# Three PSUM banks for the attention maxima, one shared bank for the transposes, and a new order of ticks, in a fused perceiver layer on one Trainium2 core

## The reference, cut to what matters

```python
Q = (q @ Wq + bq);  K = k @ Wk + bk;  V = v @ Wv + bv        # K, V: [2048, 32], shared by the heads
attn = softmax(Q K^T * scale);  out = (attn V) @ Wo + bo
```

## Time and profile before

| | us |
|---|---|
| median of 3 runs | 2032.25 |
| lowest, highest | 2029.79, 2034.01 |
| the profiled execution's own time | 2033.48 |
| its span | 2031.7 |
| PE, DVE, ACT, POOL busy | 1985.8, 1253.5, 1123.3, 1599.4 |

### The profile page before, as it was taken

One profiled execution on the slowest core, in us unless ns is written; L12 is line 12 of the kernel. 1 busy time (PEld: TensorE's weight loads), 2 busy tenths in 40 slices (PEclk: granted clock), 3 DMA queues, 4 the chain that ended last, 5 costly groups with the idle time before them and its releaser, 6 DMA issues. The chain is left out here.

```text
span 2031.7 us, 34305 instructions
## 1 busy us (share of the span) xinstructions
PE 1985.8 (98%) x12396; PEld 1310.8 (65%) x12396; DVE 1253.5 (62%) x2218; ACT 1123.3 (55%) x2093; POOL 1599.4 (79%) x1387
## 2 busy tenths in 40 slices
PE   7899999999999999999999999999999899999998
PEld 4436565656565555656565656556556899999998
DVE  5666777767777777777777777776753333333333
ACT  3656666666666666656666666666553233333333
POOL 0798999999898989899998989898995155555555
PEclk7789999999999999999999999999999899999999
DMA  6524131312213131312122121301200399999994
GB/s 227 187 104 147 44 107 38 89 49 77 79 63 89 37 89 37 108 37 88 37 87 69 55 82 58 88 32 41 78 6 17 139 366 358 355 356 354 354 363 168
DMA packets 105129, 262.23 MB, mean 129 GB/s; under 512 B 8576, under 2 KB 33920, under 8 KB 96256
## 3 DMA queue, kind: packets, MB, share of 16 engines
q1 hardware_dynamic: 96624, 236.04, 33.9%
q10 hardware_dynamic: 4752, 13.50, 1.8%
q0 software_dynamic: 3584, 10.49, 1.3%
HBM read 223.67 MB, written 25.72 MB: 123 GB/s over the span
## 5 line engine op out<-in xcount | busy, mean ns | idle before, releaser
L854 DVE TENSOR_REDUCE mpart<-bank 128x1 f32<-128x512 f32 x1024 | 670.5, 684 | 241.0 <-PE bank L434 236.6
L679 ACT ACTIVATE weights<-bank 128x512 f32<-128x512 f32 x1024 | 585.0, 597 | 238.5 <-PE bank L447 228.2
L1061 POOL TENSOR_TENSOR psum<-psum,weights 128x512 f32<-128x512 f32 x384 | 490.8, 1278 | 3.8 <-ACT weights L679 2.4
L1061 POOL TENSOR_TENSOR podd<-podd,weights 128x512 f32<-128x512 f32 x384 | 491.1, 1279 | 3.3 <-ACT weights L679 3.3
L447 PE MATMUL bank<-qT,kT 97*128 97x512 f32 x1024 | 481.9, 480 | 4.4 <-ACT weights L679 3.8
L434 PE MATMUL bank<-kT,qT 96*128 96x512 f32 x1024 | 447.0, 455 | 5.7 <-DVE mpart L854 4.1
L434 PEld LDWEIGHTS bank<-kT,qT 96*128 96x128 f32 x1024 | 198.4, 194 | 152.3 <-DVE mpart L854 99.2
L447 PEld LDWEIGHTS bank<-qT,kT 97*128 97x128 f32 x1024 | 194.3, 192 | 117.4 <-ACT weights L679 59.8
L459 PE MATMUL bank<-weights,v 128*32 128x512 f32 x2048 | 264.4, 612 | 0.0
L1317 POOL TENSOR_TENSOR w2l<-w,w2h 128x1024 fp32r<-128x1024 f32 x64 | 202.9, 3171 | 75.9 <-PE ebank L1230 54.5
L1260 ACT ACTIVATE hh<-ebank 128x512 fp32r<-128x512 f32 x64 | 38.2, 597 | 223.4 <-PE ebank L1214 223.4
(11 more groups left out here) (172 smaller groups left out, 3000.9 us busy)
## 6 DMA issues: line engine op xcount, KB each, us to landing
w<-in_w SPq DMA_DIRECT2D x48, 2048.0 KB, 20.1
w_first<-in_ctx SPq DMA_DIRECT2D x64, 1024.0 KB, 5.1
w_first<-in_w SPq DMA_DIRECT2D x16, 2048.0 KB, 11.6
dispatched<-route ACTq DMA_DIRECT2D x17, 513.0 KB, 4.2
dis<-dispatched SPq DMA_DIRECT2D x16, 513.0 KB, 3.5
qT<-qh SPq DMA_DIRECT2D x124, 64.0 KB, 4.5
xin<-in_x SPq DMA_DIRECT2D x16, 256.0 KB, 2.9
qT<-qs SPq DMA_DIRECT2D x64, 64.0 KB, 2.1
```

The source lines that it names most:

```text
L679: e.activation(p[n % NP], B_BANK[u % 2][:], ACT.Exp).then_inc(p_act.sem, 1)
L854: e.tensor_reduce(mpart[g % 2][:, 4 * (n % 4) + n // 4:4 * (n % 4) + n // 4 + 1], max_bank(b, g, n)[:], AX.X, ALU.max).then_inc(max_dve.se ...
L1061: e.tensor_tensor(acc[:], first, p[(UNITS * b + u) % NP], ALU.add).then_inc(psum_pool.sem, 1)
```

## The change

The bank of transposes is gone. Its bank (5) becomes a third bank of maxima, and the transposes of x and values take their turn in `KV_BANK`, in the same chain as keys, queries and sums. The quads of a group, before at ticks 20, 20, 33 and 37 from the group's start, are now at 21, 21, 33 and 33. All tables of ticks are new. No arithmetic, no instruction and no transfer is added or dropped; instructions change their bank, their place and their waits.

```diff
-STEADY = Prep(norm=-54, norm_pool=-47, xn=-29, xnt=-7, xnt_act=11, qproj=[28, 29, 31, 40], q_dve=38, q_act=42,
-              q_pool=43, qsend=52, kv=[21, 44, 57, 74], kvlow=[21, 45, 57, 79], kvs=[19, 44, 60, 78], kh=[23, 50,
-              65, 80], kl=[22, 52, 72, 81], vt=[59, 94], vt_act=[86, 96])
+STEADY = Prep(norm=-59, norm_pool=-40, xn=-11, xnt=8, xnt_act=13, qproj=[37, 41, 42, 48], q_dve=51, q_act=52,
+              q_pool=67, qsend=58, kv=[22, 53, 76, 86], kvlow=[23, 51, 76, 86], kvs=[26, 58, 83, 96], kh=[31, 64,
+              82, 97], kl=[32, 66, 87, 99], vt=[72, 106], vt_act=[74, 123])
+FIRST = Prep(norm=4, norm_pool=4, xn=5, xnt=6, xnt_act=7, qproj=[13, 14, 15, 16], q_dve=15, q_act=16, q_pool=18,
+             qsend=19, kv=[7, 8, 16, 40], kvlow=[8, 10, 16, 71], kvs=[8, 11, 17, 19], kh=[9, 12, 64, 80], kl=[10,
+             12, 65, 80], vt=[61, 126], vt_act=[66, 117])
-PE_AT = dict(sums=11, x1=[22, 24, 25, 27], xn2T=34, V=[38, 39, 40, 41], rkT=44, I=49, X1=52, Vn=100, oT2=103,
-             x2=[107, 109, 110, 112], xn3T=123, lg=126, loc=134, Y=[56, 62, 69, 78, 89, 96], Z=[57, 65, 73, 83, 92,
-             97], XT=[59, 68, 74, 84, 94])
+PE_AT = dict(sums=17, x1=[22, 23, 26, 30], xn2T=39, V=[43, 45, 46, 47], rkT=49, I=52, X1=53, Vn=113, oT2=116,
+             x2=[119, 120, 121, 122], xn3T=132, lg=135, loc=141, Y=[57, 70, 81, 87, 97, 106], Z=[61, 75, 84, 90,
+             100, 109], XT=[67, 76, 85, 95, 105])
+DVE_AT = dict(recip=[12, 13, 14, 15], att=17, x1=30, XT1=52, MT=53, IT=53, x2=124, lg=134, oh=135, row=139, Y=[58,
+              68, 81, 88, 96, 104], Z=[64, 69, 84, 92, 98, 104])
+POOL_AT = dict(xb=4, norm2=27, x12=30, rn=33, MT0=42, XT1=46, norm3=122, row=178)
-MAX_AT = [-37, -35, -34, -33, -32, -30, -28, -27, -24, -23, -19, -18, -14, -14, -11, -9]
-MAX_DVE = [-39, -37, -37, -36, -36, -30, -29, -28, -24, -23, -21, -21, -16, -14, -12, -12]
-MAX_TURN, MAX_ROW, PV_AT = -6, -7, [20, 20, 33, 37]
+MAX_AT = [-39, -39, -36, -35, -33, -30, -28, -27, -26, -25, -22, -19, -17, -14, -13, -12]
+MAX_DVE = [-38, -37, -35, -34, -32, -31, -30, -28, -27, -25, -21, -21, -20, -12, -12, -9]
+MAX_TURN, MAX_ROW, PV_AT = -8, -9, [21, 21, 33, 33]
...
-        A_BANK, B_BANK, PV_BANK, T_BANK, KV_BANK, P_BANK = bank[0:2], bank[2:4], bank[4], bank[5], bank[6], bank[7]
+        A_BANK, B_BANK, PV_BANK, KV_BANK, P_BANK = [bank[0], bank[1], bank[5]], bank[2:4], bank[4], bank[6], bank[7]
...
             + [(TICKS * (b - 1) + prep(b).qproj[0], b, ("q", 0)) for b in range(B)]
+            + [(TICKS * (b - 1) + prep(b).xnt, b, ("x", 0)) for b in range(B)]
+            + [(TICKS * (b - 1) + t, b, ("v", m)) for b in range(B) for m, t in enumerate(prep(b).vt)]
             + [(TICKS * (b + 1) + PE_AT["sums"], b, ("s", 0)) for b in range(B)])]
...
-            return [*A_BANK, P_BANK][n % 3] if b == g == 0 else A_BANK[(17 * g + n) % 2]
+            return A_BANK[(17 * (HG * b + g) + n) % 3]
...
+                if max_read(b, g, n) is not None:
+                    e.wait_ge(*max_read(b, g, n))
...
-                    transposes(T_BANK, lambda j: xin[:, j * P:(j + 1) * P]).then_inc(xnT_pe.sem, 1)
+                    transposes(KV_BANK, lambda j: xin[:, j * P:(j + 1) * P]).then_inc(xnT_pe.sem, 1)
...
-                    if b:
+                    if b or c == 0:
                         e.wait_ge(*kv_read(b, ("k", c)))
```

More of the change, by code:

```diff
@@ new lines @@
+LOAD_AFTER, W1_AT, ZERO_AT, ZERO_STEP = 4, 80, 34, 12
+PE_AT = dict(sums=17, x1=[22, 23, 26, 30], xn2T=39, V=[43, 45, 46, 47], rkT=49, I=52, X1=53, Vn=113, oT2=116,
+             x2=[119, 120, 121, 122], xn3T=132, lg=135, loc=141, Y=[57, 70, 81, 87, 97, 106], Z=[61, 75, 84, 90,
+             100, 109], XT=[67, 76, 85, 95, 105])
+ACT_AT = dict(xn2=36, ss=38, rk=45, xn2T=38, V=47, rkT=49, X1=52, Vn=112, oT2=113, xn3=129, xn3T=132, eg=134, X=[67,
+              77, 84, 94, 102])
+DVE_AT = dict(recip=[12, 13, 14, 15], att=17, x1=30, XT1=52, MT=53, IT=53, x2=124, lg=134, oh=135, row=139, Y=[58,
+              68, 81, 88, 96, 104], Z=[64, 69, 84, 92, 98, 104])
@@ L237, in level @@
             return (b, lv) if b < LAST else (b, 4 * lv + part)
[L241 to L251, removed]
         kv_uses = [(b, use) for _, b, use in sorted(
@@ L265, in kv_read @@
                 return kl_dve.at(before_b, c)
+            if kind in ("x", "v"):
+                return xnT_act.at(before_b) if kind == "x" else v_act.at(before_b, c)
             return q_dve.at(before_b) if kind == "q" else o_dve.at(before_b, "recip3")
@@ L272, in max_bank, with max_read @@
         def max_bank(b, g, n):
-            return [*A_BANK, P_BANK][n % 3] if b == g == 0 else A_BANK[(17 * g + n) % 2]
+            return A_BANK[(17 * (HG * b + g) + n) % 3]
+        def max_read(b, g, n):
+            before_g, before_n = divmod(17 * (HG * b + g) + n - 3, 17)
+            if before_g < 0:
+                return None
+            return max_dve.at(0, KB * before_g + before_n) if before_n < KB else mrow_act.at(0, before_g)
         lg, eg, cand = (P_BANK[:, n * E:(n + 1) * E] for n in range(3))
@@ L300, in banks_of @@
         def banks_of(b):
-            return [P_BANK] if b < LAST else [P_BANK, KV_BANK, T_BANK, PV_BANK]
+            return [P_BANK] if b < LAST else [P_BANK, KV_BANK, A_BANK[2], PV_BANK]
         def att_done(b, h):
@@ L311, in x1_bank @@
         def x1_bank(b):
-            return P_BANK if b < LAST else T_BANK
+            return P_BANK if b < LAST else A_BANK[2]
         block = ctx.enter_context(nc.Block())
@@ L438, in turn_max @@
                 e.wait_ge(*mneg_dve.at(b, g))
-                e.transpose(A_BANK[(17 * g + 16) % 2][:, 0:P], mneg[:], ident).then_inc(a_pe.sem, 1)
+                if max_read(b, g, KB) is not None:
+                    e.wait_ge(*max_read(b, g, KB))
+                e.transpose(max_bank(b, g, KB)[:, 0:P], mneg[:], ident).then_inc(a_pe.sem, 1)
             def score(b, u):
@@ L486, in prepare @@
                     e.wait_ge(*xn_act.at(b))
-                    read = turn_read(b, ("x", 0))
+                    read = kv_read(b, ("x", 0))
                     if read is not None:
                         e.wait_ge(*read)
-                    transposes(T_BANK, lambda j: xin[:, j * P:(j + 1) * P]).then_inc(xnT_pe.sem, 1)
+                    transposes(KV_BANK, lambda j: xin[:, j * P:(j + 1) * P]).then_inc(xnT_pe.sem, 1)
                 if t in prep(b).qproj:
@@ L520, in prepare @@
                     e.wait_ge(*vs_act.at(b, 2 * m + 1))
-                    e.wait_ge(*turn_read(b, ("v", m)))
-                    transposes(T_BANK, lambda j: kvs[m][:, j * P:(j + 1) * P]).then_inc(vT_pe.sem, 1)
+                    e.wait_ge(*kv_read(b, ("v", m)))
+                    transposes(KV_BANK, lambda j: kvs[m][:, j * P:(j + 1) * P]).then_inc(vT_pe.sem, 1)
             def finish(b, t):
@@ L684, in max_row @@
                     e.wait_ge(*(mrow_in[g - 2].at(b) if g >= 2 else mrow_in[g + 2].at(b - 1)))
-                e.copy(mrow[g % 2][:], A_BANK[(17 * g + 16) % 2][0:4, 0:P]).then_inc(mrow_act.sem, 1)
+                e.copy(mrow[g % 2][:], max_bank(b, g, KB)[0:4, 0:P]).then_inc(mrow_act.sem, 1)
             def out_sum(b, g):
@@ L701, in prepare @@
                     e.wait_ge(*xnT_pe.at(b))
-                    e.copy(xnT[:].rearrange("p c t -> p (c t)"), T_BANK[:]).then_inc(xnT_act.sem, 1)
+                    e.copy(xnT[:].rearrange("p c t -> p (c t)"), KV_BANK[:]).then_inc(xnT_act.sem, 1)
                 if t == prep(b).q_act:
```

14 lines of the change are left out of this document (3 added, 11 removed).

## The result

The kernel after takes 2008.73 us in the median (2003.98 to 2013.48, 4 runs), beside 2033.13 us (2029.79 to 2038.88, 4 runs) for the kernel before: a ratio of 0.9879, with a 95% interval from 0.9859 to 0.9899. The forecast was 2006. The profiled execution took 2003.98 us (span 2002.2), against 2033.48 (span 2031.7) before.

What follows compares the result with a forecast made beforehand. PE was taken to bound fourteen iterations. Terms -19.6 + 4.2 - 9.8 - 1 gave -26.2 us: 2007.3 for the profiled execution, 2006 for the median; range 1988 to 2031, the forecast's own 1998 to 2018 (chance 0.60).

Steps and rivals of the forecast that it cites:

- Quads in pairs: Third and fourth quads of each group: one merge saves 0.34 to 0.35 us, four a batch 1.4; -19.6 us over 14 iterations.
- The pair waits for its last weights: Fourth quad, now at tick 33: 0.15 us wait in two groups, 0.3 us a batch, +4.2 us; bounds 0 and 0.3 a pair.
- The third bank: Maxima behind the sums: 0.9 us wait goes, keys chunk 0 loses 0.3; net 0.7 us a batch, -9.8 us.
- The turn and the tight places: Turn at ticks 24, 56, 88, 120 gains 0.4 us a batch; tight ticks 8 to 16 cost 0.4: nothing.
- The shared bank: One bank for nine uses: cost 0 beyond chunk 0's; rival: PE stalls at keys chunk 3, 2034 to 2079 us, chance 0.13.
- POOL as the bound: POOL's work and waits for DVE: no batch under 91.4 us if waits stay, about 1997; chance 0.16, shared with larger gain.
- The prediction's sign for this rival: In the new trace: forecast wrong if a batch of POOL has no more idle time than the 6.2 us.
- Batches 0 and 1: First two batches: batch 0 left alone, within 3 us either way, its clock not steady; batch 1 forecast -1.8 us.
- The start: Before the first score: DVE can begin maxima about 31.7 instead of 33.44; -1 us, bounds -3 and +2.
- Moved DMAs and queues: Context loads at ticks 26 to 90, queries' low part at 67: nothing, hidden unless POOL is over 10 us late.
- After them come the last batch's chain and the experts, where no work is changed: Stretch after batch 15's scores: no work changed, so no difference forecast, 0 us.

Runs made afterwards that it cites:

- six more kernels: Kernel after with lone quads, two banks, own transpose bank, two banks behind the sums, first batch's old tables, or w1's load at tick 90: tails 75.70 to 76.43 us.
- the later load: Kernel after with the first expert's w1 load at SP tick 90 instead of 80, behind the row of maxima: 1995.36 us, ratio 0.9812.
- the first of the softer tail shifts: Kernel after with w1's load at tick 90 and batch 14's finish brought forward from tick 110 by a quarter of the way: 1998.03 us, ratio 0.9835.

## Why the prediction was right, and where it was not

**Quads in pairs (forecast -1.4 us a batch).** Confirmed on the new tables, and undersized: 1.93 us, of which 1.6 are four clusters and 0.3 a wait. The prediction priced a cluster from the distances of starts, which was the right reading. By the Trainium skill ("TensorEngine Tiling (Array Packing)", section Tiling Modes) changing the tiling mode drains the array; that agrees with the trace, in which each way in and out of the quads costs, and the page has no price. What the forecast left out is that a lone quad also covers a wait: on the old tables the same merge costs 1.25 us a batch. The merge can't be priced apart from the order around it.

**The pair waits for its last weights (+0.3).** Wrong: none of the 96 pairs in batches 2 to 13 has a gap inside, and they start 0.20 to 0.43 us behind what is before them, by what that is. The cost was at its lower bound. Half of the miss in the steady batch (92.0 forecast, 91.44 measured) is this one.

**The third bank (-0.7).** The place and the mechanism were right: nothing waits behind the sums, and with two banks for the four uses there PE stands 3.69 us. The keys are late by 0.12 us and not 0.3. What was wrong is the size. The term was read from what two banks cost in the old order, 0.9 us; but the old order had been laid out to live with two. What the bank is worth in the new order is 6.0 us at that place and at least 20 over a batch. These are not gains over the kernel before. They say that the new order, with its block of four reciprocals and its denser maxima, falls apart without the bank. What the bank gives the old order was not tried. As a difference between the two kernels the forecast 92.0 a batch compares with 91.44, and with no wait of pairs and the keys 0.12 late the terms give 93.80 - 1.4 - 0.9 = 91.5; with the merge at its measured 1.6 it is 91.3. That this agrees is no proof that the parts add: single edits on either order moved a batch by more than the whole change did.

**The turn and the tight places (0).** The turn's idle time of the earlier trace rows is gone, but that is worth less than 0.4: the four turns of one batch start 0.63, 0.23, 0.32 and 0.64 us behind the score ahead of them (batch 5, after), for 0.63, 0.32, 0.32 and 0.74 before, 0.2 us in all. Whether the tight places took it back was not tried apart.

**The shared bank (0; rival of 2034 to 2079).** It did not come. At the place that the rival named, the keys' last chunk, no wait for a read is seen.

**POOL as the bound (rival, 1997).** The batches stopped at 91.33 to 91.44 us in all versions that kept pairs and three banks, which is close to the 91.4 of that rival. But its condition, that POOL's waits stay, does not hold: they fell by 2 us, and PE is busy in 1095.52 of 1097.25 us. By the Trainium skill ("Perfetto Trace Analysis", section Identifying the Most-Contended Engine) the engine with the highest occupancy binds, and for TensorE the share of weight loads counts, here 62% (677.59 / 1097.25), against 93% for POOL, so that by the page POOL would bind. The case speaks for PE: the view of PE's waits lists none in these 12 batches, and work added to PE's order alone (lone quads) lengthens the batch by 1.93 us at once. No run took work off POOL, so it is not proven that a batch could fall below 91.4. The prediction's sign for this rival, a batch of POOL with no more idle time than 6.2 us, was missed by only 0.1 (6.3).

**Batches 0 and 1 (within 3, and -1.8).** Missed by 7.2 and 2.9 us. Batch 0 was left alone because its clock was unsteady. It is short in every kernel with three banks, and the granted clock in it is 0.89 for 0.80. How long PE stays at the lower level is what the forecast had no term for.

**The start (-1).** Not shown: kernels with the old start and with the new one have their first scores in the same range.

**Moved DMAs and queues (0).** This is the clear error. The paragraph went through context loads, queries and the rows' send, but not the one DMA whose wait is on a moved step: the expert weights at tick 80, behind `kv_pe` of the last chunk. The chunk went from tick 74 to 86, past the load's own tick and up to the rows' send at 87. Cost: 8.24 us of standing and 10.2 us at the lower clock behind it, 11.4 us by the experiment.

**"After them come the last batch's chain and the experts, where no work is changed" (0).** No work was changed, but ticks were. The routing chain went from 123 to 132, across the last score at 126, and lost its cover: +6.2 us in this profile, 5.5 of them ahead of the sums, and 4.1 to 4.8 by six more kernels. With the chain brought forward, the tail is 3.5 us shorter on top of the later load (72.52 for 75.97).

So the median was right to 3 us by luck: 20 us of underestimated gain met 17 us of overlooked loss.

## What to carry to other kernels

When an order is laid out anew, go through every wait that hangs on a moved step, above all those of the DMA queue, and look separately at the last iteration, where the work that covered a late chain is missing. Price a removed stall also by what the freed resource lets the rest of the order do: a buffer that saved 0.9 us in the old order carried a new one that falls apart without it. And if a merge costs time alone, that says little of its worth with the order made for it.

## What the runs showed of the hardware

A transfer of 2 KB, issued 1.7 us behind two of 2 MB on SP's queue, had its consumer start 11.1 us after the issue; issued ahead of them the consumer started 2.65 us after it, without a wait. That agrees with the Trainium skill ("DMA: Bandwidth & Descriptors", section Queues, rings and completion order), by which each DMA engine consumes the descriptors of a ring in order. No run parts the order in the ring from the shared bandwidth (421 GB/s in that stretch).

A stand of PE costs more than itself, through the clock. Behind 8.24 us the granted clock was 0.50 for 10.2 us, and the pair of quads took 3.64 us for 1.92. Behind 3.69 us, once a batch, a stretch at 0.50 held a pair of 3.09, and the batch grew by 6.0 us and not by 3.69. In the first of the softer tail shifts the clock was 0.50 for 13.6 us from within a wait of 2.54 us on, and the pair took 3.64. In batch 14 the stand of 8.24 us cost 11.4 in all.
